# The expert stage of a graph and mixture kernel: tile table, order of the tiles, and the weights' high parts

## The chip, the cores and the metric

The kernel runs on one core of a Trainium2 chip. Such a core has a matrix engine (TensorE, PE in the profile), a vector engine (VectorE, DVE), a scalar engine (ScalarE, ACT), GpSimd (POOL) and SyncE (SP), which mainly issues DMAs; 16 DMA engines move data. The metric is the device time of one execution in microseconds (us); before the change it is 3207.02 us, the median of three runs (3205.88 to 3208.4).

## The reference, cut

12500 nodes with 256 features and 200000 edges pass a graph layer and then a layer of experts. The change touches only the experts:

```
H = gelu(layernorm(x) @ W1 + b1)              # 12500 x 1024
probs = softmax(H @ Wg + bg); assign = argmax(probs)      # 8 experts
for e in range(8):
    y = H @ Wd[e] + bd[e]                     # 1024 -> 256
    out += where(assign == e, probs[:, e] * y, 0)
x = x + out
```

Each node needs the product with one expert's matrix only.

## The kernel before

The stage ahead of the experts (`gate`) computes H and the choice for each node and writes one row per node, its payload (H, x, eight gate values, its number; 1292 values, 5168 bytes), into `regions` in DRAM, grouped by expert. Two experts share one region, one growing from its low end upwards and one from its high end downwards; `sign` is +1 or -1 accordingly, and `ends` holds where each expert's rows end. `gate` also loads the experts' matrices into `w_sb`.

`experts` (L2196) walks over 105 tiles (`TTILES`, 12500 // 128 + 8) of 128 rows. A tile belongs to one expert. Tiles follow each other expert by expert, each expert's last tile partly filled; numbers past the last tile point at a block of empty rows, `NOWHERE`. Since the filling is known only at run time, a table gives each tile's first row (`row_i`) and its expert (`expert_i`), and all engines read tile numbers from it with loads into registers.

- SP (L2286 to L2305) writes 128 empty rows behind each expert's end and at `NOWHERE` (nine fills), issues the load of the bias `b_sb`, waits for the fills (`none_out`, L2292), for the table (`table_ready`), for the last rows sent by GpSimd (`sent`), and then issues one load for each tile into one of six buffers `pay` (L2303), the later ones as buffers come free.
- GpSimd (L2309 to L2321) makes four small integer tables, clears the empty rows `none`, and sends the last 512 payload rows (L2317); then it writes each tile's result out (L2326).
- DVE (L2373 to L2401) makes the table. It counts tiles of each expert with `(count + 127) >> 7`, sums them up in `cum`, and for all 105 tiles at once, against the eight experts, computes on 128 x 840 values: which experts end before the tile, the sum of that, the first row. All partitions hold the same table.
- The products are done in three parts of float32r (high x high, high x low, low x high). So each weight is split: ACT copies an expert's whole matrix into `w_hi` (L2339, 2048 values in each partition), and copies each half of it once more into `part(n)`, one of the two buffers of `hT_hi` (L2342); DVE subtracts that from the weight into `w_lo` (L2406). ACT waits for DVE's subtraction two halves back, because the buffer is used again.
- For each tile, PE turns the payload's H in eight 128x128 pieces (`turn_tile`, L2451), ACT copies the result's high part (`hT_hi`, L2353), DVE makes the low part (`hT_lo`, L2416), PE multiplies (24 matmuls, L2462), DVE adds the bias, scales and adds x (L2429 to L2435). PE's program is: turns of tile 0, turns of tile 1, wait for all split weights (L2469, L2470), products of tile 0, turns of tile 2, products of tile 1, and so on.

DVE's program is strictly in this order: table, sixteen subtractions, wait for the bias (L2407), low part of tile 0. ACT's: sixteen high parts, then tile 0. A matmul's weight operand `w[:, ds(e, 1), k, :]` has its address computed on PE's sequencer from the register `e`.

## Time and profile before

| | us |
|---|---|
| three runs, median (range) | 3207.02 (3205.88 to 3208.4) |
| the profiled execution | 3201.47 |
| its span, first to last instruction | 3199.7 |
| the expert stage within it, from its first instruction | 2752.4 to 3199.7 |
| first product of the stage on PE | 2795.47 |

Granted TensorE clock: 0.954 of full speed on average. The profile is one execution. Times in its rows count from the start of the span. The page has, first, busy time of each engine and the chain of work that ended last; the other views are answers from the same trace: instructions in order of time, the chain in order of time, sums over windows, and all instructions of one line of the kernel. An idle time before an instruction is given with what ended it.

### The profile page before, as it was taken

The numbers are of one execution on the slowest core, as the hardware profiler recorded it, in microseconds if no ns is written. First come the engines' busy times: TensorE is split into PE (matmuls) and PEld (weight loads), VectorE is DVE, ScalarE is ACT, GpSimd is POOL, SyncE is SP. The second block draws the span as 40 slices with busy tenths as digits, with TensorE's granted clock in tenths as the row PEclk, the third lists the DMA queues.
The fourth block names the chain that finished last, engine by engine and source line by source line (L and its number), as shares of the span: only waits on it lengthen the run. The fifth ranks groups of instructions, "written<-read, shape, count | busy, mean of one in ns | idle before, by whom it ended". The sixth has DMA issues, their size and how long they took to land. (4 is left out here: it accounts for less than half of the span.)

```text
span 3199.7 us, 70228 instructions
## 1 busy us (share of the span) xinstructions
PE 2829.6 (88%) x20200; PEld 2375.4 (74%) x20201; DVE 2436.9 (76%) x5978; ACT 1639.5 (51%) x3211; POOL 791.5 (25%) x733
## 2 busy tenths in 40 slices
PE   4676769999999969999999999879989998499998
PEld 2333359998989968888888887557667776399998
DVE  8888889888888858888888887666666666666665
ACT  3665148777777722222222225756666666633332
POOL 1000017777787710000000000211121112122222
PEclk9887789999999989999999999989999999699999
DMA  2332039999999979999899991003344343566664
GB/s 45 117 105 82 7 99 370 355 354 354 354 355 353 352 301 328 335 332 339 332 335 336 344 339 50 0 20 123 135 152 158 135 149 144 215 199 216 209 214 142
DMA packets 214807, 710.53 MB, mean 222 GB/s; under 512 B 28495, under 2 KB 104313, under 8 KB 189514
## 3 DMA queue, kind: packets, MB, share of 16 engines
q1 hardware_dynamic: 130778, 405.55, 37.1%
q0 software_dynamic: 83952, 304.02, 24.6%
q8 instruction: 40, 0.66, 0.1%
q14 instruction: 37, 0.30, 0.0%
HBM read 383.91 MB, written 340.05 MB: 226 GB/s over the span
## 5 line engine op out<-in xcount | busy, mean ns | idle before, releaser
L1409 PE MATMUL coll_ps_sum<-coll_rows,coll_hot 128*128 128x256 f32 x2940 | 657.4, 381 | 29.0 <-DVE coll_hot L1344 28.9
L1409 PEld LDWEIGHTS coll_ps_sum<-coll_rows,coll_hot 128*128 128x128 f32 x2940 | 550.9, 191 | 105.9 <-DVE coll_hot L1344 31.3
L915 POOL DMA_INDIRECT messages<-send_msg,send_to x448 | 525.3, 1173 | 165.5 <-issue 139.9
L1060 PE MATMUL send_ps_msg<-send_parts,send_pick 128*128 128x256 f32 x3584 | 538.9, 293 | 1.1
L1100 ACT ACTIVATE send_msg<-send_ps_msg 128x1024 f32<-128x1024 f32 x448 | 459.2, 1025 | 140.5 <-PE send_ps_msg L1060 138.9
L1060 PEld LDWEIGHTS send_ps_msg<-send_parts,send_pick 128*128 128x128 f32 x3584 | 456.2, 190 | 12.4 <-issue 4.8
L1344 DVE TENSOR_SCALAR coll_hot<-coll_nodes,coll_rows 128x128 f32<-128x128 f32 x1470 | 393.3, 340 | 4.1 <-issue 1.8
L963 DVE TENSOR_SCALAR send_pick<-send_ps_local,edges_down 128x512 fp32r<-128x512 f32 x448 | 334.1, 746 | 8.4 <-PE send_ps_local L1048 1.5
L1463 ACT ACTIVATE nodes_hid<-coll_ps_turned 128x256 f32 (+1 forms) x98 | 37.6, 383 | 552.2 <-PE coll_ps_turned L1241 552.2
L2006 DVE TENSOR_TENSOR gate_act_lo<-gate_act_h,gate_act_hi 128x512 fp32r<-128x512 f32 x200 | 140.1, 701 | 172.8 <-ACT gate_act_hi L1915 162.2
L1538 POOL CAST lin_x_hi<-lin_hT 128x1024 fp32r<-128x1024 f32 x25 | 28.9, 1158 | 941.2 <-ACT lin_hT L1674 888.0
L2462 PE MATMUL exp_ps_y<-exp_w_hi,exp_hT_hi 128*128 x840 | 244.5, 291 | 6.5 <-DVE exp_hT_lo L2416 6.5
L2353 ACT ACTIVATE exp_hT_hi<-exp_ps_t 128x1024 fp32r<-128x1024 f32 x105 | 107.7, 1025 | 260.5 <-PE exp_ps_t L2451 259.9
L2462 PE MATMUL exp_ps_y<-exp_w_lo,exp_hT_hi 128*128 x840 | 236.0, 281 | 0.0
L2462 PE MATMUL exp_ps_y<-exp_w_hi,exp_hT_lo 128*128 x840 | 235.9, 281 | 0.0
L1858 POOL DMA_INDIRECT regions<-gate_pay,gate_where_i x96 | 92.4, 963 | 500.3 <-DVEq L2042 478.4
L1914 ACT ACTIVATE gate_act_h<-gate_ps_h,gating_b 128x512 f32<-128x512 f32 x200 | 138.3, 691 | 134.4 <-PE gate_ps_h L2163 134.2
L591 DVE TENSOR_REDUCE sort_place<-sort_banks 128x8 f32<-128x784 f32 x224 | 185.7, 864 | 12.0 <-PE sort_banks L766 10.8
L1455 ACT ACTIVATE coll_high<-coll_rows 128x256 fp32r<-128x256 f32 x392 | 166.5, 496 | 52.7 <-DMA coll_rows<-messages 49.7
L1048 PE MATMUL send_ps_local<-send_localT,edges_spread 128*128 128x128 f16 x1792 | 179.0, 223 | 8.0 <-DVE send_pick L963 4.6
L2326 POOL DMA_INDIRECT out_dram<-exp_res,exp_token x105 | 103.2, 983 | 326.8 <-DVE exp_res L2435 322.2
L2163 PE MATMUL gate_ps_h<-gate_xnT_hi,gate_w_hi 128*128 128x512 f32 x400 | 176.7, 442 | 2.6 <-DVE gate_xnT_lo L1999 2.6
(324 smaller groups left out, 5819.0 us busy)
## 6 DMA issues: line engine op xcount, KB each, us to landing
coll_rows<-messages SPq DMA_DIRECT2D x98, 1300.0 KB, 7.3
coll_rows<-messages SPq DMA_DIRECT2D x98, 1170.0 KB, 7.3
exp_pay<-regions SPq DMA_DIRECT2D x105, 646.0 KB, 4.2
send_window<-node_rows SPq DMA_DIRECT2D x112, 128.0 KB
node_rows<-sort_xn SPq DMA_DIRECT2D x25, 512.0 KB, 5.0
coll_own<-node_rows SPq DMA_DIRECT2D x98, 128.0 KB, 4.2
sort_xt<-in_x_dram SPq DMA_DIRECT2D x24, 512.0 KB, 4.3
layers_w<-in_x_dram SPq DMA_DIRECT2D x24, 384.0 KB
```

Source lines behind the costliest of these rows:

```text
L591: dve.tensor_reduce(place[:, n % BATCH, 2 * a0:2 * a1].rearrange("p (a u) -> p a u", u=2), ranks[:, a0:a1, 0:2 * NB].rearrange("p a (b u) ...
L915: pool.indirect_dma_start(out=runs_out[:, :], out_offset=bass.IndirectOffsetOnAxis(ap=to[:, s, q:q + 1], axis=0), in_=msg[:, s, q, :, :].r ...
L963: dve.tensor_scalar(pick[:, q * RUN:(q + 1) * RUN, :], ps_local[:, q % 2], k.down[:, 0:1], None, ALU.is_equal).then_inc(pick_ready, 1)
L1048: ins = pe.matmul(ps_local[:, q % 2, a, :], k.spread[:, q * RUN + a, :], localT[:, d, :], start=True, stop=True)
L1060: ins = pe.matmul(ps_msg[:, q % 2, a, :], pick[:, q * RUN + a, :], parts[:, s % 2, part, :], start=(part == 0), stop=(part == 1))
L1100: act.activation(msg[:, s, q, :, 0:D], ps_msg[:, q % 2, :, :], ACT.Copy).then_inc(kept, 1)
L1344: ins = dve.tensor_scalar(hot_of(s, j), nodes[:], node_of(u, j), weight_of(u, j), ALU.is_equal, ALU.mult)
L1409: ins = pe.matmul(ps_sum[:, s, 0:D], hot_of(s, j), features(u, j), start=(j == CX), stop=(j == CJ - 1))
L1455: ins = act.activation(high[:, s, j, :], features(u, j), ACT.Copy, scale=weight_of(u, j))
L2006: dve.tensor_tensor(act_lo[:, k % 2, :], act_h[:, k % 2, :], act_hi[:, k % 2, :].bitcast(F32), ALU.subtract).then_inc(act_lo_ready, 1)
L2163: ins = pe.matmul(ps_h[:, k % 2, :], w[:, q, k * P:(k + 1) * P], a[:, s, q, :], start=(q == 0 and w is w_hi and a is xnT_hi), stop=(q == D ...
L2462: ins = pe.matmul(ps_y[:, s, 0:D], h[:, s, k, :], w[:, ds(e, 1), k, :].rearrange("p o f -> p (o f)"), start=(k == 0 and h is hT_hi and w i ...
```

## The change

Three things are changed, all in `experts`.

1. The table is made with one tile in each partition: tile numbers come from an iota along partitions, and the comparisons with the eight experts are on 128 x 8 values. Two columns result (`table`: first row, expert), which two matmuls with the identity turn into rows in PSUM (`ps_y`), and two copies bring to `row_i` and `expert_i`, now in one partition.
2. Only full tiles are counted (`count >> 7`); they come first, expert by expert, and behind them one partly filled tile for each of the eight experts. SP waits for the fills only before tile 84 (`WHOLE` = 14 rounds of six tiles, a number of full tiles that there are always).
3. `w_hi` becomes two tensors, one for each half of the 1024 rows; ACT writes each half once, DVE subtracts from it directly, and `part`, its semaphore and ACT's waits for DVE are gone.

The diff, cut to its core:

```
-        w_hi = m.sb("w_hi", [P, NE, KC, D], F32R)
+        w_hi = [m.sb(f"w_hi{h}", [P, NE, KC // 2, D], F32R) for h in range(2)]
...
+        WHOLE = (N - NE * (P - 1)) // P // U
...
-        def part(n):
-            return hT_hi[:, n % 2].rearrange("p k q -> p (k q)")
+        def high_of(n):
+            return w_hi[n % 2][:, n // 2].rearrange("p k f -> p (k f)")
...
                 sp.dma_start(b_sb[:].rearrange("p e f -> p (e f)"), bd.rearrange("e f -> (e f)").partition_broadcast(P)).then_inc(w_in, 16)
-                sp.wait_ge(none_out, 16 * (NE + 1))
                 sp.wait_ge(table_ready, 1)
                 for s in range(2):
                     sp.wait_ge(sent[s], 16 * CH * (LAST // 2 + 1 - s))
...
-                all_tiles(sp, tile)
+                for u in range(U):
+                    tile(u, u, 0)
+                with sp.Fori(1, WHOLE, 1) as i:
+                    for u in range(U):
+                        tile(U * i + u, u, i)
+                sp.wait_ge(none_out, 16 * (NE + 1))
+                with sp.Fori(WHOLE, FULL, 1) as i:
+                    for u in range(U):
+                        tile(U * i + u, u, i)
+                for u in range(TTILES - U * FULL):
+                    tile(U * FULL + u, u, FULL)
...
-                pool.iota(tile_i[:], [[1, TTILES]], base=0, channel_multiplier=0).then_inc(iotas, 1)
+                pool.iota(tile_i[:], [[0, 1]], base=0, channel_multiplier=1).then_inc(iotas, 1)
...
                 for n in range(2 * NE):
-                    if n % 2 == 0:
-                        act.activation(w_hi[:, n // 2], w_sb[:, n // 2], ACT.Copy).then_inc(w_hi_ready, 1)
-                    if n >= 2:
-                        act.wait_ge(w_split, n - 1)
-                    act.activation(part(n), half_of(w_sb, n), ACT.Copy).then_inc(part_ready, 1)
+                    act.activation(high_of(n), half_of(w_sb, n), ACT.Copy).then_inc(w_hi_ready, 1)
...
-                steps.link(dve.tensor_scalar(cum[:], cum[:], float(P - 1), None, ALU.add))
...
-                steps.link(dve.tensor_tensor(wide[:], across(tile_f), along(cum), ALU.is_ge))
+                steps.link(dve.tensor_scalar(wide[:], cum[:], tile_f[:, 0:1], None, ALU.is_le))
                 steps.link(dve.tensor_reduce(expert[:], wide[:], AX.X, ALU.add))
+                steps.link(dve.tensor_tensor(behind[:], tile_f[:], cum[:, NE - 1:NE], ALU.subtract))
+                steps.link(dve.tensor_scalar(spare[:], behind[:], -float(NE), None, ALU.add))
+                steps.link(dve.scalar_tensor_tensor(spare[:], behind[:], 0.0, spare[:], ALU.is_ge, ALU.mult))
+                steps.link(dve.tensor_tensor(expert[:], expert[:], spare[:], ALU.add))
+                steps.link(dve.tensor_scalar(past_wide[:], cum[:], tile_f[:, 0:1], float(P), ALU.min, ALU.mult))
...
+                dve.tensor_scalar(table[:, 1:2], expert[:], float(NE - 1), None, ALU.min).then_inc(tiles_found, 1)
+                dve.wait_ge(tiles_turned, 1)
+                dve.sem_inc(dve_turn, 1)
+                steps.link(dve.tensor_copy(row_i[:], ps_y[0:1, 0, 0:TTILES]))
+                steps.link(dve.tensor_copy(expert_i[:], ps_y[0:1, 1, 0:TTILES]))
                 dve.sem_inc(table_ready, 1)
                 for n in range(2 * NE):
-                    dve.wait_ge(w_hi_ready, n // 2 + 1)
-                    dve.wait_ge(part_ready, n + 1)
+                    dve.wait_ge(w_hi_ready, n + 1)
                     dve.sem_inc(dve_turn, 1)
-                    dve.tensor_tensor(half_of(w_lo, n), half_of(w_sb, n), part(n).bitcast(F32), ALU.subtract).then_inc(w_split, 1)
+                    dve.tensor_tensor(half_of(w_lo, n), half_of(w_sb, n), high_of(n).bitcast(F32), ALU.subtract).then_inc(w_split, 1)
...
+                pe.wait_ge(tiles_found, 1)
+                for a in range(2):
+                    ins = pe.matmul(ps_y[0:1, a, 0:TTILES], table[0:TTILES, a:a + 1], c.ident[0:TTILES, 0:TTILES], start=True, stop=True)
+                ins.then_inc(tiles_turned, 1)
...
-                        for h, w in ((hT_hi, w_hi), (hT_hi, w_lo), (hT_lo, w_hi)):
+                        high = w_hi[k // (KC // 2)][:, ds(e, 1), k % (KC // 2), :].rearrange("p o f -> p (o f)")
+                        low = w_lo[:, ds(e, 1), k, :].rearrange("p o f -> p (o f)")
+                        for h, w in ((hT_hi, high), (hT_hi, low), (hT_lo, high)):
```

## Rows read from the trace of the kernel before

**Rows 1.** The page: the chain that ended last by line, and the loads' median landing

```profile
PE exp_ps_y L2462 9%; PE exp_ps_t L2451 3%; ACT exp_hT_hi L2342 0%; ACT exp_w_hi L2339 0%; DVE exp_w_lo L2406 0%; DVE exp_hT_lo L2416 0%; DVE exp_cum L2384 0%; DVE exp_sign L2374 0%; DVE exp_wide L2391 0%; DVE exp_past_wide L2393 0%; DVE exp_wide L2396 0%; DVE exp_wide L2395 0%; DVE exp_past_wide L2394 0%; DVE exp_row L2397 0%; DVE exp_expert L2392 0%
...
exp_pay<-regions SPq DMA_DIRECT2D x105, 646.0 KB, 4.2
```

**Rows 2.** Windows: start:end, length, busy us of each engine (instructions), granted clock, DMA share, GB/s

```profile
2756.00:2776.00 20.00, 0.00 (x0) 0.00 (x0) 16.87 (x27) 9.90 (x9) 2.56 (x3) 0.50 1.02 398
...
2782.00:2786.00 4.00, 1.94 (x8) 1.56 (x8) 2.67 (x3) 4.00 (x4) 0.00 (x0) 0.50 0.88 278
2786.00:2792.00 6.00, 1.97 (x8) 1.57 (x8) 3.33 (x4) 6.00 (x6) 0.00 (x0) 0.50 1.00 409
...
2801.00:2802.00 1.00, 1.00 (x9) 1.00 (x8) 0.73 (x4) 0.00 (x0) 0.00 (x0) 0.75 0.00 0
2802.00:3180.00 378.00, 378.00 (x3267) 378.00 (x3266) 246.46 (x509) 123.56 (x306) 100.27 (x102) 1.00 0.68 207
```

**Rows 3.** Instructions of PE by time: start, us, engine, line, names, shapes, count [idle before]

```profile
2783.72 1.94 PE L2451 MATMUL exp_ps_t<-all_ident,exp_pay 128*128 128x128 f32 x8 [33.90 <-DMA exp_pay<-regions]
2787.01 1.97 PE L2451 MATMUL exp_ps_t<-all_ident,exp_pay 128*128 128x128 f32 x8 [1.35 <-DMA exp_pay<-regions]
2795.47 0.57 PE L2462 MATMUL exp_ps_y<-exp_w_hi,exp_hT_hi 128*128 x1 [6.49 <-DVE exp_hT_lo L2416]
```

**Rows 4.** The same view of DVE

```profile
2757.97 0.17 DVE L2390 CAST exp_index<-exp_index_i 128x8 f32<-128x8 int32 x1
2758.17 1.11 DVE L2391 TENSOR_TENSOR exp_wide<-exp_tile_f,exp_cum 128x840 f32<-128x840 f32 x1
...
2765.96 0.27 DVE L2399 TENSOR_TENSOR exp_row_i<-exp_row,exp_tile_f 128x105 int32<-128x105 f32 x1
...
2766.77 4.81 DVE L2406 TENSOR_TENSOR exp_w_lo<-nodes_hid,exp_hT_hi 128x1024 fp32r<-128x1024 f32 x4 [0.29 <-DVE exp_expert_i L2400]
...
2791.56 2.36 DVE L2406 TENSOR_TENSOR exp_w_lo<-nodes_hid,exp_hT_hi 128x1024 fp32r<-128x1024 f32 x2 [1.33 <-ACT exp_hT_hi L2342]
2794.10 1.23 DVE L2416 TENSOR_TENSOR exp_hT_lo<-exp_ps_t,exp_hT_hi 128x1024 fp32r<-128x1024 f32 x1 [0.18 <-ACT exp_hT_hi L2353]
```

**Rows 5.** The same view of ACT

```profile
2754.22 1.99 ACT L2342 ACTIVATE exp_hT_hi<-nodes_hid 128x1024 fp32r<-128x1024 f32 x2
...
2768.03 2.19 ACT L2342 ACTIVATE exp_hT_hi<-nodes_hid 128x1024 fp32r<-128x1024 f32 x2 [10.02 <-DVE exp_w_lo L2406]
```

**Rows 6.** The same view of SP, DMA issues from its queue

```profile
2767.91 1.33 SPq L2290 DMA_DIRECT2D regions<-exp_none  x1
2769.28 1.24 SPq L2291 DMA_DIRECT2D exp_b_sb<-in_L_ffn_bd_dram  x1
2780.13 23.55 SPq L2303 DMA_DIRECT2D exp_pay<-regions  x7
```

**Rows 7.** Landings, by line: first the last fill (L2290), then the bias (L2291)

```profile
DMA to landing us min/median/max: 11.5/11.5/11.5
...
DMA to landing us min/median/max: 12.4/12.4/12.4
```

**Rows 8.** All of L2317, the last sends: duration in ns, first and last start

```profile
L2317 POOL DMA_INDIRECT regions<-gate_pay,gate_where_i x4: 957/962/1028, 2754.3 to 2758.2; - x4
...
DMA to landing us min/median/max: 5.1/8.8/11.5
```

**Rows 9.** The chain in order of time: start, us, what

```profile
2795.47 5.48 PE exp_ps_y L2462 x24
2802.15 2.83 PE exp_ps_y L2462 x24
```

**Rows 10.** Register work of PE's sequencer in one tile, by line, 2999.9 to 3003.6: ns, starts

```profile
L2462 PEldq FUSED_REGOPS  x8: 46/46/46, 3001.0 to 3002.8; - x8
L2462 PEldq ALU_OP  x8: 32/32/32, 3001.2 to 3002.9; - x8
...
L2455 PEldq FUSED_REGOPS  x2: 42/96/151, 3000.1 to 3000.6; - x2
```

More of the change, by code:

```diff
@@ L2205, in experts @@
         b_sb = m.sb("b_sb", [P, NE, D])
-        w_hi = m.sb("w_hi", [P, NE, KC, D], F32R)
+        w_hi = [m.sb(f"w_hi{h}", [P, NE, KC // 2, D], F32R) for h in range(2)]
         none = m.sb("none", [P, PAY])
-        tile_i = m.sb("tile_i", [P, TTILES], I32)
-        tile_f = m.sb("tile_f", [P, TTILES])
-        row = m.sb("row", [P, TTILES])
-        expert = m.sb("expert", [P, TTILES])
-        row_i = m.sb("row_i", [P, TTILES], I32)
-        expert_i = m.sb("expert_i", [P, TTILES], I32)
+        tile_i = m.sb("tile_i", [P, 1], I32)
+        tile_f = m.sb("tile_f", [P, 1])
+        behind = m.sb("behind", [P, 1])
+        spare = m.sb("spare", [P, 1])
+        table = m.sb("table", [P, 2])
+        expert = m.sb("expert", [P, 1])
+        row_i = m.sb("row_i", [1, TTILES], I32)
+        expert_i = m.sb("expert_i", [1, TTILES], I32)
         index_i = m.sb("index_i", [P, NE], I32)
         index = m.sb("index", [P, NE])
-        wide = m.sb("wide", [P, TTILES, NE])
-        past_wide = m.sb("past_wide", [P, TTILES, NE])
+        wide = m.sb("wide", [P, NE])
+        past_wide = m.sb("past_wide", [P, NE])
         first = m.sb("first", [P, NE], I32)
@@ L2241, in experts @@
         table_ready = m.sem("table_ready")
+        tiles_found = m.sem("tiles_found")
+        tiles_turned = m.sem("tiles_turned")
         pay_in = [m.sem(f"pay_in{s}") for s in range(SLOTS)]
@@ L2244, in experts @@
         w_hi_ready = m.sem("w_hi_ready")
-        part_ready = m.sem("part_ready")
         w_split = m.sem("w_split")
@@ L2364, in _ @@
                 steps = Steps(dve, steps_sem)
-                shape = [P, TTILES, NE]
-                def across(tiles):
-                    return tiles[:].unsqueeze(2).to_broadcast(shape)
-                def along(numbers):
-                    return numbers[:].unsqueeze(1).to_broadcast(shape)
                 dve.wait_ge(iotas, 4)
@@ L2395, in _ @@
-                steps.link(dve.tensor_tensor(wide[:], across(expert), along(index), ALU.is_equal))
-                steps.link(dve.tensor_tensor(wide[:], wide[:], past_wide[:], ALU.mult))
-                steps.link(dve.tensor_reduce(row[:], wide[:], AX.X, ALU.add))
-                steps.link(dve.tensor_scalar(tile_f[:], expert[:], float(NE), float(NOWHERE), ALU.is_equal, ALU.mult))
-                steps.link(dve.tensor_tensor(row_i[:], row[:], tile_f[:], ALU.add))
-                steps.link(dve.tensor_scalar(expert_i[:], expert[:], float(NE - 1), None, ALU.min))
+                steps.link(dve.tensor_tensor(behind[:], tile_f[:], cum[:, NE - 1:NE], ALU.subtract))
@@ new lines, in _ @@
+                steps.link(dve.tensor_tensor(past_wide[:], past_wide[:], offset[:], ALU.add))
+                steps.link(dve.tensor_scalar(wide[:], index[:], expert[:, 0:1], None, ALU.is_equal))
+                steps.link(dve.tensor_tensor(wide[:], wide[:], past_wide[:], ALU.mult))
+                steps.link(dve.tensor_reduce(table[:, 0:1], wide[:], AX.X, ALU.add))
+                steps.link(dve.tensor_scalar(spare[:], expert[:], float(NE), float(NOWHERE), ALU.is_ge, ALU.mult))
+                steps.link(dve.tensor_tensor(table[:, 0:1], table[:, 0:1], spare[:], ALU.add))
@@ L2459, in multiply @@
                     for k in range(KC):
-                        for h, w in ((hT_hi, w_hi), (hT_hi, w_lo), (hT_lo, w_hi)):
-                            ins = pe.matmul(ps_y[:, s, 0:D], h[:, s, k, :], w[:, ds(e, 1), k, :].rearrange("p o f -> p (o f)"),
-                                            start=(k == 0 and h is hT_hi and w is w_hi), stop=(k == KC - 1 and h is hT_lo))
+                        high = w_hi[k // (KC // 2)][:, ds(e, 1), k % (KC // 2), :].rearrange("p o f -> p (o f)")
+                        low = w_lo[:, ds(e, 1), k, :].rearrange("p o f -> p (o f)")
+                        for h, w in ((hT_hi, high), (hT_hi, low), (hT_lo, high)):
+                            ins = pe.matmul(ps_y[:, s, 0:D], h[:, s, k, :], w,
+                                            start=(k == 0 and h is hT_hi and w is high), stop=(k == KC - 1 and h is hT_lo))
                     ins.then_inc(y_done, 1)
@@ L2468, in _ @@
                 turn_tile(1, 1, 0)
-                pe.wait_ge(w_hi_ready, NE)
+                pe.wait_ge(w_hi_ready, 2 * NE)
                 pe.wait_ge(w_split, 2 * NE)
```

5 lines of the change are left out of this document (1 added, 4 removed).

## The prediction

> **What bounds the kernel now.** I read the page first for its chain and span [rows 1]: only the last stage is in the chain, and in it PE's products (L2462) and turns (L2451) are 12% of 3199.7 us. The windows of that stage then show two parts [rows 2]. From 2802 us on PE is busy 378.00 of 378.00 us at a granted clock of 1.00: nothing in this change makes that part shorter, unless it changes PE's own stream. Before it, from 2752 to 2796, PE does two tiles' turns and waits. So the question is which wait ends last before the first product at 2795.47 us [rows 3].
>
> Three chains run to it. DVE builds the tile table until 2766.5, subtracts sixteen halves of the weights until 2793.9, and makes the first tile's low part from 2794.10 to 2795.33; PE starts 0.14 us later [rows 4]. ACT holds DVE: it runs ahead, stops 10.02 us for DVE's first subtraction, and from then on each pair of halves costs it two part copies and one whole copy, so that DVE idles 1.33 us before each of the last six pairs [rows 4, 5]. The third chain is the data. SP issues nine fills and the bias, the last fill lands 11.5 us after 2767.91, at 2779.4, and only then the first load goes out, at 2780.13 [rows 6, 7]. Its tile reaches PE at 2783.72, the next at 2787.01 [rows 3], both well before 2795.47. So **DVE's chain ends last now, by some eight us, and the data's is next**.
>
> **The table.** It is 8.60 us from L2391 to the first subtraction (2758.17 to 2766.77), because seven operations of 840 elements take over 1 us each [rows 4]. They become fifteen operations of 1 to 8 elements; such a one starts 0.20 us before the next (L2390 at 2757.97, L2391 at 2758.17) [rows 4], so 15 x 0.2 = 3.1 us. New is the turn of the table into a row: two products on PE. The trace has no product like them. The nearest are the 128x128 turns at the same low clock, 1.94/8 = 0.24 us each [rows 3]: from below two of them, 0.5 us, from above all eight, 1.9 us; I take 0.7 us, since there are two and they have 105 columns, plus 0.1 us for each hand-over (DVE to PE takes 0.14 us, 2795.33 to 2795.47 [rows 3, 4]). Two copies to integers of 105 elements go by L2399, 0.27 us, so 0.6 us with their starts. With 0.2 us to the first subtraction: 3.1 + 0.7 + 0.2 + 0.6 + 0.2 = 4.8 us. One addition (L2378) goes, 0.2 us. The first subtraction moves from 2766.8 to about 2762.8 (between 2762.6 and 2764.0).
>
> **The weights' high parts.** ACT loses the eight copies of 2048 elements and keeps sixteen of 1024, which follow each other at 1.99/2 = 1.0 us [rows 5]. They have their own storage, so no wait for DVE: 2752.4 + 16 = 2768.4 us. DVE's subtractions follow each other at 1.20 us (four in 4.81 us) [rows 4], start later and run slower, so ACT never holds them: 2762.8 + 15 x 1.2 + 1.2 = 2782.0 us. That is 11.9 us earlier than 2793.92. DVE then waits for the bias (L2407), which lands 12.4 us after 2769.28, at 2781.7 [rows 6, 7]: the same moment, nothing lost. If DVE were the only chain the first product would come at 2782.0 + 0.2 + 1.2 + 0.1 = 2783.5, a gain of 12.0 us.
>
> **The loads.** SP no longer waits for the fills before the first 84 tiles. It goes on from the bias at 2770.5; the table is ready, and the four sends, the last issued at 2758.2 and the slowest landing after 11.5 us, are down by 2769.7 [rows 8]. So the first load is issued about 9.6 us sooner. But the queue is not empty. The core's 16 DMA engines are busy 1.02 of the time from 2756 to 2776, at 398 GB/s [rows 2]: the nine fills, the sends and the bias keep them so, and the loads are behind them in SP's own queue. The fills land before the bias, in the order of issue, so I let the loads land behind the bias too. Then load 0 is not down 9.6 us sooner: a load is 646 KB, or 661.5 kB, at the 409 GB/s of the loads alone [rows 2] 1.6 us. 2781.7 + 1.6 = 2783.3, against just before 2783.72 now. Load 1 gains more: 2784.9 against 2787.0, if the share of 0.88 and the 278 GB/s between 2782 and 2786 [rows 2] come from loads being issued too late, which is how I read it; if they don't, load 1 comes 3.3 us behind load 0, at 2786.6.
>
> The Trainium skill, page "DMA: Bandwidth & Descriptors", section "Queues, rings and completion order", says that on each DMA engine descriptors are consumed in ring order. It speaks against this part of the change; by it the early issue is worth a fraction of a us for load 0. By that rule the trace agrees as far as it goes: the bias, behind nine fills, landed 12.4 us after its issue [rows 7].
>
> **What is late next.** Load 0 at 2783.3; PE turns it in 1.94 us from 2783.4 to 2785.4 (low clock) [rows 3]; ACT copies 1024 values in 1.0 us, DVE's low part comes 0.18 us later, takes 1.23 us, and 0.14 us later PE starts [rows 3 to 5]: 2785.4 + 1.0 + 0.2 + 1.2 + 0.1 = 2787.9. PE's program has the turns of tile 1 first: load 1 at 2784.9, turns from 2785.4 to 2787.3, so they just fit; with load 1 at 2786.6 they end at 2788.6 and the first product comes at 2788.8. I take 2788.1, a gain of 7.4 us (down to 6.3, if both loads land as now and the turns end near 2789.1, up to 7.6). DVE has 4.5 us in hand, so that a slower table costs nothing here; the cover of the table and of the subtractions is the data.
>
> **PE's clock.** Tile 0 runs 24 products at the low level, 1.2 GHz: 5.48 us, against 2.83 us at 2.4 GHz [rows 9]. The clock rose in the window 2801 to 2802 (mean 0.75) [rows 2], some 6 us after PE's restart, before which it had stood still for 6.49 us [rows 3]. Now that gap shrinks to 0.5 to 1 us. If the rise still takes 6 us from the first product, nothing more is gained; if it counts from the first turns, it comes up to 4.5 us sooner, and in 4.5 us 45% are won back: 2.0 us. I take 0.7 us.
>
> **Order of tiles, and the rest.** The number of tiles stays 105, each takes PE 3.70 us, turns and products (from 2802 to 3180 there are 3267 instructions of 32 a tile, 102.1 tiles in 378.00 us, 3.70) [rows 2]; only which expert comes when changes. SP's wait for the fills stands now before tile 84, 84 x 3.7 = 310 us later: nothing. Behind that wait only later loads are queued. The tail after PE is the same.
>
> **PE's addresses.** One part does touch all 105 tiles. The high and the low weights had the same stride, so one register operation of 46 ns and one of 32 ns served the three products of a k [rows 10]. With the high weights in two tiles of half the stride, the offset can't be shared between high and low. Bounds: nothing, or each product computing its own (24 x 46 = 1.10 us for 8 x 78 = 0.62 us now, 0.48 us more a tile). I take 46 for 32 ns in four to eight of the k, 0.06 to 0.11 us. How much is free: PE's sequencer starts on a tile's expert number at 3000.1, on its products at 3001.0, on the last k at 3002.8 [rows 10]; a k takes it 1.8/7 = 0.26 us, of which 0.18 us are six instructions, 0.03 us each, so the turns' sixteen take 0.48 us. With 0.1 us for a wait that is 3000.1 to 3003.65, 3.55 of 3.70 us, and the rows may hold waits of its own: at least 0.15 us are free, and the addition is hidden, just.
>
> **Sum, against the profiled execution (3201.47 us, span 3199.7).** 7.4 + 0.7 = 8.1 us less: 3193.4. The median of the runs is 5.5 us above that execution; I carry that over: 3207.0 - 8.1 = 3198.9 us.
>
> **The rivals.**
> (a) *The loads land as before*: their pace, not their issue, sets the first product. Gain 6.3 us, no clock: 3200.7. For it: nine fills before them in the queue, the DMA at 1.02. Against: the dip to 0.88 when the loads were issued late. Chance 0.20.
> (b) *The loads pass the fills*: by the median of all loads, 4.2 us [rows 1], load 0 would be down at 2774.8, and DVE's chain would set the start: 12.0 us and 1 us of clock: 3194.0. Against it: the bias's landing. Chance 0.07.
> (c) *PE's sequencer becomes the bound* (slower than before). It decides from 0.15 us more a tile; at 0.48 us more it costs 0.33 x 105 = 35 us, less the 8.1: 3234; at 0.23 us it just cancels the gain. For it: the small slack. Against: PE never waits from 2802 on, though the sequencer also closes a loop every six tiles. Chance 0.06.
> (d) *The change doesn't do what it says*: a wait I don't see keeps the first tiles behind the fills, or the start-up stays at 2793 or later, as when ACT's copies and DVE's subtractions slow each other by a third (16 x 0.4 = 6.4 us, of which 4.5 are covered). Gain 2 to 5 us: 3203.5. Chance 0.07.
> The forecast, loads in ring order and 7 to 10 us gained, has 0.60.
>
> **How the numbers follow.** 0.2% of this kernel is 6.4 us, about what a measurement can tell from no change: the bound lies at 3200.6. The forecast's own range, with 2 us of scatter in the medians, is 3195.5 to 3201. It falls below the bound in some nine of ten cases (0.55), (b) always (0.07), (a) in two of ten (0.04): faster 0.66. Same: 0.05 + 0.16 + 0.07 and 0.01 of (c), 0.29. Slower: 0.05. The range of eight in ten takes in (a), most of (b) and half of (d): 3192 to 3204.
>
> **What would show it.** Right: the table's row copies near 2762.5; sixteen ACT copies without a gap until 2768.4; DVE's subtractions without a gap until about 2782; the first load issued near 2770.6 yet down only near 2783.3, over 12 us later; DVE idle for some 4.5 us between; the first product at about 2788; tiles at 3.70 us. Wrong: turns before 2780 (b); tile 1's turns starting at 2787 (a); idle time of PE between products (c); a first product behind 2790 (d).

## The result, and the profile after

| | before | after |
|---|---|---|
| runs compared here, median (range), us | 3208.14 (3204.43 to 3213.15), 19 runs | 3202.03 (3197.47 to 3206.39), 19 runs |
| span of the profiled execution, us | 3199.7 | 3201.5 |

The ratio is 0.9981, with an interval from 0.9974 to 0.9988: **6.1 us less** (3.8 to 8.3). The profiled execution of the changed kernel came to this stage 8.5 us later than that of the kernel before: the stage's first instruction, ACT's first copy of a weight, is at 2760.91 us there and at 2752.40 before. The stages ahead of it are the same and vary by so much: in ten of the traces used below, these two among them, this stage begins between 2752.4 and 2760.9 us. Everything below is therefore counted from the stage's first instruction, written T+.

The chain of the page, after, answers to [rows 1]. ACT's copies and DVE's subtractions are gone from its front; the loads' transfer (DMA exp_pay) and SP's queue stand there:

```profile
PE exp_ps_y L2474 9%; PE exp_ps_t L2461 3%; DMA exp_pay<-regions 0%; SPq L2292 0%; SPq L2293 0%; SPq L2295 0%; SPq L2294 0%; DVE exp_hT_lo L2422 0%; POOL exp_none L2326 0%; SPq L2305 0%; ACT exp_hT_hi L2360 0%; POOL out_dram L2339 0%; DVE exp_res L2441 0%; DVE exp_res L2435 0%; DVE exp_prob L2440 0%
```

DVE, ACT, SP's queue and PE by time, after (as [rows 3 to 6]; start, us, engine, line, names, shapes, count, idle before):

```profile
2766.18 0.17 DVE L2388 CAST exp_index<-exp_index_i 128x8 f32<-128x8 int32 x1
...
2769.33 0.15 DVE L2403 TENSOR_SCALAR exp_table<-exp_expert 128x1 f32<-128x1 f32 x1
2770.55 0.26 DVE L2406 CAST exp_row_i<-exp_ps_y 1x105 int32<-1x105 f32 x1 [1.06 <-PE exp_ps_y L2451]
...
2771.35 18.25 DVE L2412 TENSOR_TENSOR exp_w_lo<-nodes_hid,exp_w_hi 128x1024 fp32r<-128x1024 f32 x16 [0.26 <-DVE exp_expert_i L2407]
2795.80 1.23 DVE L2422 TENSOR_TENSOR exp_hT_lo<-exp_ps_t,exp_hT_hi 128x1024 fp32r<-128x1024 f32 x1 [6.20 <-ACT exp_hT_hi L2360]
```

```profile
2760.91 15.25 ACT L2351 ACTIVATE exp_w_hi<-nodes_hid 128x1024 fp32r<-128x1024 f32 x16 [6.39 <-PEq L1813]
```

```profile
2777.67 1.37 SPq L2295 DMA_DIRECT2D exp_b_sb<-in_L_ffn_bd_dram  x1
2780.51 8.48 SPq L2306 DMA_DIRECT2D exp_pay<-regions  x6
```

```profile
2769.54 0.86 PE L2451 MATMUL exp_ps_y<-all_ident,exp_table 105*1 105x105 f32 x4 [11.22 <-DVE exp_table L2403]
2792.57 3.43 PE L2461 MATMUL exp_ps_t<-all_ident,exp_pay 128*128 128x128 f32 x16 [22.17 <-DMA exp_pay<-regions]
2797.18 0.38 PE L2474 MATMUL exp_ps_y<-exp_w_hi,exp_hT_hi 128*128 x1 [1.18 <-DVE exp_hT_lo L2422]
```

The reader sees four things. The subtractions start at 2771.35, T+10.4, and sixteen of them run in one piece of 18.25 us to T+28.7 (before: T+14.4 to T+41.5, in pairs with gaps [rows 4]). Then DVE stands still for 6.20 us: it is no longer last. PE's turns wait for the DMA of the loads until 2792.57, T+31.7, 0.3 us later than before [rows 3]. And the first product is at 2797.18, T+36.3, against T+43.1: **6.8 us sooner**.

Two more changes lie behind that. Tile 0's products are quicker, and all later ones slower. The chain in order of time, after (as [rows 9]; the chain counts tile 1 from the end of the turns before it, 0.25 us behind the start of its first product), and then one steady window before and after (as [rows 2]: start:end, length, busy us of each engine (instructions), granted clock, DMA share, GB/s):

```profile
2797.18 3.13 PE exp_ps_y L2474 x24
...
2801.18 2.85 PE exp_ps_y L2474 x24
```

```profile
2802.00:3168.00 366.00, 366.00 (x3163) 366.00 (x3162) 238.76 (x492) 119.93 (x297) 97.32 (x99) 1.00 0.69 211
```

```profile
2802.00:3168.00 366.00, 366.00 (x3140) 366.00 (x3139) 237.04 (x490) 119.06 (x296) 96.38 (x98) 1.00 0.69 211
```

Tile 0's 24 products took 5.48 us before [rows 9] and take 3.13 now. With that, tile 1's first product is 9.5 us sooner (T+40.0 against T+49.5). But in the same 366 us, PE busy throughout at a clock of 1.00, it gets through 3140 instructions in the place of 3163. From one tile's first product to the next (the period), the mean is 3.733 us, against 3.706 before (unrounded 3.7333 and 3.7055). Over the tiles behind tile 1 that **gives 2.8 us back**. PE's last product comes at T+426.48 against T+433.13, 6.65 us sooner, and the interval of the measured difference (3.8 to 8.3) holds that. The forecast had no such loss.

### The profile page after: what moved, and what is told of

Its sections match the earlier page's. It is cut to its first block and busy times, and to the rows that moved or that the text cites. A ratio compares the mean times of both kernels' runs of the same rounds, so it can differ in the third digit from the quotient of the medians.

```text
span 3201.5 us, 70235 instructions
## 1 busy us (share of the span) xinstructions
PE 2830.3 (88%) x20204; PEld 2371.8 (74%) x20205; DVE 2429.7 (76%) x5984; ACT 1626.8 (51%) x3203; POOL 790.8 (25%) x733
## 5 line engine op out<-in xcount | busy, mean ns | idle before, releaser
L1409 PE MATMUL coll_ps_sum<-coll_rows,coll_hot 128*128 128x256 f32 x2940 | 657.6, 381 | 29.1 <-DVE coll_hot L1344 28.7
L1409 PEld LDWEIGHTS coll_ps_sum<-coll_rows,coll_hot 128*128 128x128 f32 x2940 | 550.4, 191 | 107.0 <-DVE coll_hot L1344 34.6
```

The source lines that it names most:

```text
L1409: ins = pe.matmul(ps_sum[:, s, 0:D], hot_of(s, j), features(u, j), start=(j == CX), stop=(j == CJ - 1))
```

## The experiments

`b_two_high`, `b_longer_address`, `b_four_high` and `b_warm` ran on a chip on which the stages ahead of this one took some 160 us longer, in the kernel before too (3368.45 us); only times within the stage are used of them. This table is from the traces of all kernels, one execution each, counted from the stage's first instruction. The last column has the time of the whole kernel, and behind it that of the kernel before as timed with it; with numbers of runs where there was more than one (medians):

| kernel | load 0 / load 1 landed | subtractions end | first product | tile 1's first product | period | last product | time, us / before |
|---|---|---|---|---|---|---|---|
| before | 31.2 / 34.6 | 41.5 | 43.07 | 49.5 | 3.706 | 433.1 | - |
| after | 31.5 / 33.1 | 28.7 | 36.27 | 40.0 | 3.733 | 426.5 | 3202.03 (19) / 3208.14 (19) |
| b_two_high | 31.2 / 34.0 | 42.1 | 43.64 | 49.7 | 3.706 | 433.3 | 3368.55 / 3368.45 |
| b_longer_address | 31.8 / 33.6 | 41.5 | 43.08 | 49.3 | 3.706 | 433.0 | 3372.88 / 3368.45 |
| b_four_high | 31.3 / 34.1 | 43.2 | 44.75 | 50.2 | 3.706 | 433.8 | 3372.03 / 3368.45 |
| b_moved_64 | 31.3 / 34.3 | 41.5 | 43.07 | 49.4 | 3.756 | 438.1 | 3207.20 / 3206.37 (11) |
| b_warm | 31.6 / 34.0 | 41.5 | 43.08 | 46.8 | 3.706 | 430.4 | 3363.36 / 3368.45 |
| b_table | 31.4 / 34.1 | 36.8 | 38.40 | 43.7 | 3.722 | 429.0 | 3204.72 / 3200.61 |
| b_high_once | 31.5 / 34.3 | 32.6 | 36.24 | 41.3 | 3.706 | 424.9 | 3201.06 / 3206.37 (11) |
| a_wait_fills | 31.4 / 34.2 | 28.7 | 36.10 | 41.1 | 3.733 | 427.5 | 3201.77 / 3200.61 |
| a_same_places | 31.1 / 32.7 | 28.7 | 35.84 | 39.6 | 3.706 | 423.2 | 3195.34 / 3200.61 |
| a_same_timed (same code) | 30.9 / 32.5 | 28.7 | 35.68 | 40.9 | 3.706 | 424.5 | 3196.61 (7) / 3206.37 (11) |
| a_loads_first | 16.1 / 19.9 | 28.7 | 30.32 | 36.3 | 3.733 | 422.8 | 3191.08 / 3200.61 |
| a_all_three | 15.9 / 18.5 | 28.7 | 30.26 | 36.2 | 3.706 | 419.8 | 3191.88 (5) / 3206.37 (11) |

The stage's own start varies by up to 8.5 us from one execution to another, so a single time of the whole kernel can't show a difference of this size: `b_table` was 4.1 us slower than the kernel timed with it although its last product is 4.1 us sooner within the stage, and `b_moved_64` was 0.8 us slower although its last product is 5.0 us later. Where only one run was timed, the readings below rest on the trace.

### What makes each tile longer

My first theory after the result was the address work on PE's sequencer, since the two kernels' rows differ there, as the prediction had said they would (one line's register work in a tile, after and then `b_two_high`; before it was 8 of 46 ns [rows 10]):

```profile
L2474 PEldq FUSED_REGOPS  x12: 46/46/46, 3001.5 to 3003.4; - x12
```

```profile
L2465 PEldq FUSED_REGOPS  x12: 46/46/46, 3168.1 to 3170.0; - x12
```

**b_two_high**, the kernel before with the cut of `w_hi` alone:

```
-w_hi = m.sb("w_hi", [P, NE, KC, D], F32R)
+w_hi = [m.sb(f"w_hi{h}", [P, NE, KC // 2, D], F32R) for h in range(2)]
...
+high = w_hi[k // (KC // 2)][:, ds(e, 1), k % (KC // 2), :]
```

(ACT's copy of an expert's whole matrix becomes two, one into each tensor.)

> The kernel before with w_hi cut into two tensors of four k each, as in the changed kernel, and nothing else of the change. In the traces of the two kernels a tile took 3.706 us before and 3.733 us after, and PE's sequencer ran 12 long and 4 short register instructions a tile (46 and 32 ns) in the place of 8 and 8. Theory: the cut of w_hi alone makes the longer tile, since w_hi and w_lo no longer have one stride and share no address work. Then the period here is 3.73 us (3.725 to 3.74), with 12 long and 4 short instructions, and about 103 x 0.027 = 2.8 us are lost. Rival: the longer period comes from the order of the tiles, from the new row of the table or from something else in the changed kernel; then it stays at 3.706 us here.

Measured: the 12 long instructions are there, and the period is 3.706 us. The theory fell.

**b_longer_address**, no tensor changed, longer address work:

```
+e_low = e if k % 2 else (e + NE * (k + 1)) % NE
...
-w[:, ds(e, 1), k, :]
+w[:, ds(e_low if w is w_lo else e, 1), k, :]
```

> The kernel before, all tensors in their places and of their shapes, but the index of w_lo is (e + 8 (k + 1)) mod 8 for even k, which is e again: the compiled program then has 12 long and 4 short register instructions a tile on PE's queue, as the changed kernel has, four of them longer still. Theory one: the number and length of the register instructions on PE's sequencer make the longer period, wherever the weights lie. Then the period is 3.73 us or more. Theory two: it is where the two halves of w_hi lie in memory, or their shapes, and register work hides behind the matmuls; then it stays at 3.706 us.

Its rows show 12 of them, up to 114 ns long:

```profile
L2462 PEldq FUSED_REGOPS  x12: 46/46/114, 3166.5 to 3170.0; - x12
```

The period is 3.706 us. Register work of this size on PE's sequencer hides behind the products; the prediction had reckoned so for a smaller amount.

**b_four_high**, `w_hi` in four tensors:

```
+w_hi = [m.sb(f"w_hi{h}", [P, NE, KC // 4, D], F32R) for h in range(4)]
```

> As the run with two tensors, but w_hi is cut into four tensors of two k each: 10 long and 6 short register instructions a tile, so 2 long ones more than before where the cut in two has 4 more. Theory one (register work counts): half of the extra period, about 3.719 us. Theory two (a cut tensor or its place counts): at least as long as with two tensors, 3.733 us or more.

Period 3.706 us: both theories fell with this one too. (The smaller copies on ACT delayed the start by 1.7 us.)

So neither the form of the weights nor their addresses did it. Within a tile, the trace shows every product from the third on 117 to 119 ns behind the one before it in the kernel before (a few of 116, 121 or 122), and in the changed kernel a repeating pattern, 120, 119, 115, 118, 122 ns in three of the six tiles of the loop, 119 and 121 in two others, the same in every round. The operations by form in those 366 us (line, engine, operation, names, count | busy us, mean ns of one | idle us; `after`, then before) show which are slower:

```profile
L2474 PE MATMUL exp_ps_y<-exp_w_hi,exp_hT_lo 128*128 x785 | 221.7, 282 | 0.0
...
L2461 PE MATMUL exp_ps_t<-all_ident,exp_pay 128*128 128x128 f32 x784 | 101.5, 272 | 0.0
```

```profile
L2462 PE MATMUL exp_ps_y<-exp_w_hi,exp_hT_lo 128*128 x792 | 221.4, 280 | 0.0
L2451 PE MATMUL exp_ps_t<-all_ident,exp_pay 128*128 128x128 f32 x787 | 102.1, 272 | 0.0
```

The products are 2 ns longer, the turns are not. What the products read beside the weights is `hT_hi` and `hT_lo`, and these had moved: the table's tensors lie ahead of them in each partition's memory, and the smaller table moved `hT_hi`, `hT_lo`, `res` and `pay` down by 8256 bytes, from 172960 to 164704.

**a_same_places**, the changed kernel with one line more:

```
+room = m.sb("room", [P, 2064])
 hT_hi = m.sb("hT_hi", [P, 2, KC, P], F32R)
```

> The changed kernel with 8256 unused bytes a partition ahead of hT_hi, so that hT_hi, hT_lo, res and pay lie where they lay before (the smaller table had moved them down by that much); nothing else differs. In the traces every product of a tile follows the one before it by 118 ns before, and by a pattern of 115 to 122 ns after (mean 119.5), the same in every tile of a place in the loop; neither two tensors for w_hi nor longer address instructions did that to the kernel before. Theory: the place of the operands in memory sets the pattern. Then the period is 3.706 us and the products 118 ns apart, 2.8 us less than the changed kernel has in the steady part. Rival: it is the two instructions more ahead of PE's loop, or the order of the tiles; then the period stays at 3.73 us.

The period is 3.706 us, and the products are 118 ns apart again; its window has as many instructions as that of the kernel before:

```profile
2802.00:3168.00 366.00, 366.00 (x3163) 366.00 (x3163) 238.70 (x496) 120.15 (x297) 96.64 (x99) 1.00 0.69 212
```

**b_moved_64**, the kernel before with the four tensors 64 bytes further (`hT_hi` at 173024):

```
+room = m.sb("room", [P, 16])
```

> The kernel before with 64 unused bytes a partition ahead of hT_hi, so that hT_hi, hT_lo, res and pay lie 64 bytes further, and nothing else. The move of 8256 bytes by which the changed kernel differs is 64 more than 8192. Theory: the place of the operands alone sets the pitch of the products (the changed kernel with its old places had 118 ns and a period of 3.706 us again). Then it is enough here to lengthen the period to 3.72 to 3.75 us, in a kernel that has nothing of the change. Rival: it takes the place and the shift of the program together, or only certain larger moves matter; then the period stays at 3.706 us.

```profile
2802.00:3168.00 366.00, 366.00 (x3121) 366.00 (x3120) 235.68 (x489) 118.73 (x293) 95.47 (x97) 1.00 0.68 209
```

The period is 3.756 us, 0.050 more (3.72 to 3.75 was expected), and PE's last product is 5.0 us later within the stage. A place alone, in a kernel that has nothing of the change, costs nearly as much as the whole change brings. The place is the cause. The turns read `pay`, which moved too, and didn't become longer; but **which of the four tensors it is and why 64 bytes matter stays open**: `room` moved all of them, and no run parted them.

**a_same_timed**, the code of `a_same_places`, timed:

> The changed kernel with the old places of hT_hi, hT_lo, res and pay, timed. The changed kernel took 0.9981 of the time of the kernel before (6.1 us less) with a steady part that is 2.8 us longer. Theory: that is given back, so 8.5 to 9.5 us less than before (ratio 0.9970 to 0.9974). Rival: what the trace shows of the period is no time of the kernel, since the end of the chain waits elsewhere; then the ratio stays at 0.998.

3196.61 us against 3206.37 before (medians), ratio 0.9968 (0.9957 to 0.9979): 10.3 us less (6.7 to 13.8). The interval holds the expected 8.5 to 9.5 us. It overlaps a little with that of the changed kernel (0.9974 to 0.9988), so the 2.8 us rest on the traces more than on these times.

### What each part gives at the start

**b_table**, the kernel before with the table along partitions alone (the order of the tiles as before, so with `+ float(P - 1)` and without the lines on `behind`):

```
-steps.link(dve.tensor_tensor(wide[:], across(tile_f), along(cum), ALU.is_ge))
+steps.link(dve.tensor_scalar(wide[:], cum[:], tile_f[:, 0:1], None, ALU.is_le))
...
+ins = pe.matmul(ps_y[0:1, a, 0:TTILES], table[0:TTILES, a:a + 1], c.ident[0:TTILES, 0:TTILES], start=True, stop=True)
```

> The kernel before with the table made with tiles along partitions and turned by PE, and nothing else: the tiles in their old order, loads behind the fills, high parts made twice. Expected against the kernel before, within the stage: subtractions begin 3.9 us sooner (14.4 to 10.4 us from the stage's start), and so does the end of their chain with ACT, from 41.5 to about 37.6; the first product moves from 43.1 to about 39.2. Rival (the loads are what is late): load 0 still lands at 31.2 and the first product stays where it was. On the period of the tiles: here hT_hi lies at yet another place (32 bytes below that of the changed kernel) with PE's loop as far into its program as in the changed kernel; if the place or the shift of the program makes the longer period, it is over 3.71 us, if the order of the tiles or the cut of w_hi does, it is 3.706.

The first product moves to T+38.4, 4.7 us sooner (3.9 expected). Subtractions begin at T+9.7, which is more than the table gives in the changed kernel, since that one has four operations more in all for its order of the tiles. The period is 3.722 us, with `hT_hi` at 164672: a third place, a third period.

**b_high_once**, the kernel before with the high parts made once:

```
-if n % 2 == 0:
-    act.activation(w_hi[:, n // 2], w_sb[:, n // 2], ACT.Copy).then_inc(w_hi_ready, 1)
-if n >= 2:
-    act.wait_ge(w_split, n - 1)
-act.activation(part(n), half_of(w_sb, n), ACT.Copy).then_inc(part_ready, 1)
+act.activation(high_of(n), half_of(w_sb, n), ACT.Copy).then_inc(w_hi_ready, 1)
```

> The kernel before with the high parts made once (w_hi in two tensors, 16 copies on ACT in the place of 24, subtractions from w_hi) and nothing else: table and loads as before. Theory: the subtractions begin at 14.4 us from the stage's start as before, but run without a gap, 16 x 1.14 = 18.3 us, and end at 32.7 (41.5 before); that is ahead of load 1, which lands at 34.1 to 34.6, so that the loads are late now and the first product comes at 36.1 to 36.8 us, as in the changed kernel: this edit alone gives nearly the whole gain, and the table's 3.9 us are worth nothing beside it. Period 3.706 us, since nothing moves hT_hi. Rival: the subtractions still wait for the copies or for each other, and end at 37 us or later.

PE and DVE by time in it:

```profile
2791.84 1.94 PE L2444 MATMUL exp_ps_t<-all_ident,exp_pay 128*128 128x128 f32 x8 [34.21 <-DMA exp_pay<-regions]
2794.57 1.97 PE L2444 MATMUL exp_ps_t<-all_ident,exp_pay 128*128 128x128 f32 x8 [0.80 <-DMA exp_pay<-regions]
2796.45 0.58 PE L2457 MATMUL exp_ps_y<-exp_w_hi,exp_hT_hi 128*128 x1
```

```profile
2795.07 1.23 DVE L2409 TENSOR_TENSOR exp_hT_lo<-exp_ps_t,exp_hT_hi 128x1024 fp32r<-128x1024 f32 x1 [2.29 <-ACT exp_hT_hi L2347]
```

The first product is at T+36.2, as in the changed kernel, and DVE still stood still for 2.29 us. One of the three edits gives the whole 6.8 us, because the data is last from there on; the table's 4 us lie in DVE's idle time. And as nothing moves `hT_hi`, its last product is at T+424.9, 1.6 us sooner than that of the changed kernel with all three edits.

**a_wait_fills**, the changed kernel without the edit to the loads:

```
+sp.wait_ge(none_out, 16 * (NE + 1))
 sp.wait_ge(table_ready, 1)
```

> The changed kernel with the old wait for all fills put back ahead of the first load, and nothing else: it undoes the part of the change that moves the loads. Theory: the loads' packets stand behind the fills' on the same queues anyway (in the changed kernel load 0 was issued 8.1 us sooner and landed 0.3 us later within the stage, 4.4 us behind the last fill), so that not waiting gains next to nothing: first product at 36.7 to 37.0 us from the stage's start against 36.3, the kernel slower by 0.2 to 0.7 us. Rival: the earlier issue is worth what it looks like; then load 0 lands 3.5 us or more later than in the changed kernel (at 35 us), and the first product comes at 39 us or later.

The first load is issued at T+27.5 in the place of T+19.6, and load 0 lands at T+31.4, where it landed at T+30.9 to T+31.5 in the three executions with the earlier issue. The first product is at T+36.1, earlier than the expected 36.7 to 37.0, and between 0.2 us sooner and 0.4 us later than in those three. What is lost is load 1, 1.0 to 1.6 us later; here too PE turned tile 1 until the product began, and tile 1's first product is 0.2 to 1.5 us later than in those. So the early issue is worth at most 0.4 us at the first product and 0.2 to 1.5 us behind it, and in the latter tile 0's clock, which differs from one execution to the next (below), is mixed in.

**a_loads_first**, the changed kernel with the fills behind the first six loads:

```
 sp.dma_start(b_sb[:].rearrange("p e f -> p (e f)"), ...)
 sp.wait_ge(table_ready, 1)
...
 for u in range(U):
     tile(u, u, 0)
+sp.wait_ge(none_set, 1)
+for e in range(NE):
+    end = sp.value_load(ends[0:1, e:e + 1], min_val=0, max_val=NOWHERE - P)
+    sp.dma_start(regions[ds(end, P), :], none[:]).then_inc(none_out, 16)
+sp.dma_start(regions[NOWHERE:NOWHERE + P, :], none[:]).then_inc(none_out, 16)
```

> The changed kernel with the nine fills issued behind the first six loads: the fills' packets no longer stand ahead of the loads'. The bias goes first. The first six tiles are full ones, so the fills aren't needed for them. Theory: the queue of the fills is what is late in the changed kernel. Then load 0 lands at 20 to 23 us from the stage's start (31.5 in the changed kernel), the turns come at once behind it, and the subtractions are last: they end at 28.7, first product about 30.1 us, 6 us sooner than in the changed kernel, and the kernel 5 to 6 us faster than it. Rival: the loads are late for another reason (the sends into the same rows, the wait for them, the memory itself); then load 0 lands no more than 3 us sooner and the first product moves by 3 us at most.

SP's queue and PE by time:

```profile
2752.34 0.36 SPq L2290 DMA_DIRECT2D exp_b_sb<-in_L_ffn_bd_dram  x1
2764.75 5.83 SPq L2301 DMA_DIRECT2D exp_pay<-regions  x6
```

```profile
2768.60 1.94 PE L2461 MATMUL exp_ps_t<-all_ident,exp_pay 128*128 128x128 f32 x8 [6.74 <-DMA exp_pay<-regions]
2772.27 1.97 PE L2461 MATMUL exp_ps_t<-all_ident,exp_pay 128*128 128x128 f32 x8 [1.74 <-DMA exp_pay<-regions]
2782.66 0.58 PE L2474 MATMUL exp_ps_y<-exp_w_hi,exp_hT_hi 128*128 x1 [8.43 <-DVE exp_hT_lo L2422]
```

Load 0 lands 3.7 us after its issue at T+12.4; behind the fills it took 11.9 us. It is down 15 us sooner, well ahead of the 20 to 23 expected, the last of the sends 6.3 us sooner too (T+11.1 against T+17.3). Of these 15.4 us 7.2 are the earlier issue (after, SP first issued ten transfers, and the last send landed later), and 8.2 the shorter way from issue to landing. What the data waited for was the transfers ahead of it, as the theory has it: the fills, and with them the bias, which this edit moved to the front too (it is down at T+4.6); no run parts the two. (The Trainium skill, "DMA: Bandwidth & Descriptors", section "Queues, rings and completion order", has each DMA engine take descriptors in ring order; by that rule the two landings of load 0 agree.) The subtractions are last again, and the first product is at T+30.3 (30.1 expected). Of those 6 us only 3.7 arrive at tile 1: PE had stood still for 8.43 us and ran tile 0 at the low clock (5.39 us for its products). In time it was one run, 3191.08 us beside 3200.61 before.

### The clock at tile 0

**b_warm**, the kernel before with turns that nobody reads:

```
 turn_tile(1, 1, 0)
+for n in range(28):
+    pe.transpose(ps_y[:, 1, 0:P], pay[:, 0, n % KC * P:(n % KC + 1) * P], c.ident[:])
```

> The kernel before with 28 turns of a loaded tile into an unread part of PSUM, behind the turns of tiles 0 and 1 and ahead of the waits for the weights: TensorE works through most of the 6.5 us in which it stood idle before tile 0's first product. Nothing that is computed changes. Theory: what the changed kernel gained beyond the earlier first product (tile 0's products took 5.48 us before and 3.13 us after, at granted clocks of one level and the other) comes from the shorter idle time ahead of them. Then tile 0's products take 2.8 to 3.2 us here, tile 1's first product comes 2.3 to 3.3 us earlier after tile 0's, and the kernel is 2 to 3 us faster, with the first product where it was. Rival: the clock at tile 0 depends on something else (the load of the whole chip, the time since the stage began); then tile 0's products still take about 5.5 us.

Its windows: while the added turns run, while PE is idle behind them, and in tile 0's products:

```profile
2955.00:2956.90 1.90, 1.90 (x18) 1.90 (x17) 0.74 (x1) 1.90 (x3) 0.00 (x0) 0.92 0.87 354
2957.30:2960.00 2.70, 0.00 (x0) 0.00 (x0) 2.44 (x3) 2.44 (x4) 0.00 (x0) 1.00 0.02 7
2960.00:2963.00 3.00, 2.93 (x25) 2.93 (x25) 1.23 (x1) 1.27 (x5) 0.00 (x0) 1.00 0.00 0
```

The clock rose in the added turns, stayed up in 2.83 us of idle time, and tile 0's products took 3.09 us. The first product stayed at T+43.1, tile 1's came 2.7 us sooner, and so did PE's last. So idle time ahead of tile 0 had a price here, 2.7 us. But the changed kernel's gain of that size was partly luck: `a_same_places` and `a_same_timed` are the same code with the same 0.96 us of idle time, and their windows from 2791.80 to 2795.00 (in this order) show

```profile
2791.80:2795.00 3.20, 2.96 (x25) 2.96 (x26) 1.32 (x2) 1.43 (x6) 0.00 (x0) 1.00 0.76 309
```

```profile
2791.80:2795.00 3.20, 3.18 (x15) 3.18 (x16) 1.23 (x1) 1.22 (x5) 0.00 (x0) 0.50 0.73 297
```

one at 1.00, one at 0.50. In the one the level rose at T+35.2, ahead of the products, in the other at T+39.1, near their end; tile 1 came 3.74 and 5.23 us behind tile 0. (The Trainium skill, "TensorE: Matmul & The Clock Gate", section "What's actually happening", says that the monitor runs freely and isn't reset by the kernel, so that the moment of the rise varies; by it these two agree.)

**a_all_three**: fills behind the first loads, the old places, and 40 added turns:

```
+room = m.sb("room", [P, 2064])
...
 turn_tile(1, 1, 0)
+for n in range(40):
+    pe.transpose(ps_y[:, 1, 0:P], pay[:, 0, n % KC * P:(n % KC + 1) * P], c.ident[:])
```

> The changed kernel with three edits: the fills behind the first six loads, the old places of hT_hi, hT_lo, res and pay, and 40 turns of a loaded tile into an unread part of PSUM between the turns of tile 1 and the waits for the weights, so that TensorE works while the last subtractions run. From the runs before: first product at 30.3 us from the stage's start (43.1 before), tile 0's products at the higher clock in 2.8 to 3.2 us (5.1 to 5.5 us without the turns), tile 1's first product at 34.0 to 34.3 us (49.5 before, 36.3 with the fills moved alone), period 3.706. In all 15 to 16 us less than before, ratio 0.9950 to 0.9954. Rival: the clock falls in the idle time that remains (about 2.5 us) or the added turns are late themselves; then tile 1's first product comes at 36 us, and the kernel is 13 us faster than before.

PE by time:

```profile
2779.82 5.11 PE L2483 MATMUL exp_ps_y<-all_ident,exp_pay 128*128 128x128 f32 x40
2789.74 0.57 PE L2475 MATMUL exp_ps_y<-exp_w_hi,exp_hT_hi 128*128 x1 [4.82 <-DVE exp_hT_lo L2423]
```

and its windows in the added turns and in tile 0's products:

```profile
2782.00:2783.00 1.00, 1.00 (x11) 1.00 (x10) 1.00 (x2) 0.00 (x0) 0.00 (x0) 1.00 1.22 254
...
2790.00:2792.00 2.00, 2.00 (x10) 2.00 (x11) 0.46 (x1) 0.00 (x0) 0.00 (x0) 0.50 1.02 411
```

The rival came true: against `a_loads_first` the added turns gained nothing at tile 1, and PE's last product is 13.3 us sooner than before. At the high clock the 40 turns were over in 5.11 us, 4.82 us of idle time were left, the level fell 2.9 us into them (from 1.00 to 0.50 at T+28.3), and tile 0's products took 5.29 us. Tile 1's first product is at T+36.2; longer added work was not tried. Even so its last product is the earliest of all kernels here (T+419.8): 3191.88 us against 3206.37 (medians), **ratio 0.9952** (0.9938 to 0.9965), 15 us less (11 to 20). The changed kernel's interval (0.9974 to 0.9988) lies wholly above that one.

## Why the prediction was right, and where it wasn't

The forecast was 8.1 us less and 3198.9 us; measured are 6.1 us less (3.8 to 8.3) and 3202.03. That lies in the range of eight in ten (3192 to 3204) and outside the forecast's own range (3195.5 to 3201); of the 3.1 us that it is off, 1.1 are the kernel before, whose median over 19 runs is 3208.14 and not 3207.02. A gain of more than 6.4 us, which had the higher chance (0.66), isn't what the medians show, though the interval holds it. Point by point, in T+:

- **The table**: first subtraction forecast at 10.4, was 10.45. DVE stood still for 1.06 us for PE's part, 0.16 over the estimate (0.7 + 0.2); the fifteen small operations took the 3.1 us of the forecast (whose product 15 x 0.2 is 3.0), and those ahead of them ended 0.1 us sooner than reckoned.
- **The high parts**: ACT's copies ran 15.25 us without a gap (forecast 16). The subtractions took 1.14 us each, not 1.20, and ended at 28.7 (forecast 29.6). (One reading was loose: before, DVE idled 1.52 us ahead of one pair and 1.33 ahead of five, not 1.33 ahead of six.)
- **The loads**: forecast to be issued at 18.2 and down at 30.9 and 32.5. They were issued at 19.6 and down at 31.5 and 33.1 (30.9 and 32.5 in `a_same_timed`). That the early issue would be worth a fraction of a us for load 0 was right: `a_wait_fills` shows -0.2 to 0.4 us, `a_loads_first` that it was the transfers in front. The bias landed at 30.0 (forecast 29.3), ahead of its need, and load 0 1.6 us behind it, as the sum has it.
- **What is late next**: the data, with DVE idle; forecast 4.5 us of idle time, was 6.20. First product forecast 35.7, was 36.3, 35.8 and 35.7 in three executions (in the first, the profiled one, load 0 was down 0.6 us behind the forecast): gain 7.4 forecast, 6.8 to 7.4 found.
- **PE's clock**: mis-sized. I took 0.7 us with a bound of 2.0; tile 1 gained 2.7 us more than tile 0 in the profiled pair, and 1.2 and 2.7 in the two executions of the same code. The term is no fixed size but a matter of chance, between about 1 and 2.7 us here; 2.7 is what the whole of tile 0 costs at the low level against the high one (5.48 less 2.83 [rows 9]). The old start varies too: tile 1 came 6.4 us behind tile 0 in the profiled pair, and 5.4 to 6.3 us in the four other traces with all of the old idle time.
- **PE's addresses**: right that they hide; the longer instruction came in four of the k. Rival (c), the sequencer as the bound, is excluded for this amount by `b_two_high` and `b_longer_address`.
- **The step that failed** is "only which expert comes when changes", each tile 3.70 us. The list of what touches all 105 tiles held the instructions of PE's stream and not the place of what they read. The smaller table moved `hT_hi` and the three tensors behind it, and the period grew from 3.7055 to 3.7333 us: 2.8 us given back.

The sum as it was: 6.8 + 2.7 - 2.8 = 6.7 us in the profiled pair, against 7.4 + 0.7 = 8.1. Of the terms the start is 0.6 us short, the clock 2.0 us over and the tiles 2.8 us worse than nothing. Errors of opposite sign nearly cancelled; that the total came so close is luck. Without the move of the four tensors it would have been 8.6 to 9.9 us (`a_same_timed`, `a_same_places`, by PE's last product).

Rival (a) was nearer than its 0.20: load 0 did land as before. It failed on load 1, which came about 1.4 us sooner. Rival (b), loads passing the fills, is excluded by load 0 in the changed kernel. `a_loads_first` shows what it would have been worth: its first product at T+30.3. Rival (d) is excluded by the first load's issue at T+19.6 and the first product at T+36.3.

## What to carry to other kernels

Ask of each edit whether the chain it shortens is still last once the others are made: here one of three gave all of the start, and dropping the wait for a queued transfer moved the first product by 0.4 us at most, while taking the transfers out of the loads' way moved it by six us. When a change resizes a tensor, look at what lies behind it in memory, and compare the steady window's instruction count of the two traces before believing that a loop is untouched; a line of padding that puts the operands back showed it here. Keep an account of the matrix engine's idle time ahead of a burst: filling it paid where the filling reached to within 2.83 us of the burst, and not where 4.82 us were left (one execution each).

## What was not expected of the hardware

- **PE's pace depends on where its operands lie**, in steps as small as 64 bytes. Period of a tile by the first byte of `hT_hi`: 172960: 3.706 us (nine traces of eight kernels, before among them, equal to 0.001 us); 164672: 3.722; 164704: 3.733 (three traces, equal to 0.001 us); 173024: 3.756. (Only the pairs `a_same_places` and after, `b_moved_64` and before, differ in the place alone.) The Trainium skill, "SBUF — State Buffer", section "SBUF: two separate sides", has PE's reads never wait for anyone; no run here shows whom, if anyone, the products wait for, only that the same work at another place takes 1 to 2 ns more for each product (0.028 and 0.050 us over 23 steps).
- The granted level of TensorE's clock stayed at 1.00 through 2.83 us of idle time and fell 2.9 us into another stretch (and 3.0 us into one in `b_longer_address`); the same code met tile 0 at either level.
- DMAs queued ahead also delayed those of another queue: with the fills gone from the front, GpSimd's last send was down at T+11.1 in the place of T+17.3. (The bias went first there, so that both it and the fills had changed place.)
